# Attention rows held per group of four heads, and row maxima from 32-row products on a quarter of the array each

## The chip, the cores and the metric

The kernel runs on one core of one Trainium2 chip. Its time is the device time of one execution in microseconds. The program is one launch: eight transformer-like layers are computed one after the other on an activation of 2048 tokens by 128 channels that stays on chip.

## The reference

The input `x` is (1, 2048, 128). Each layer adds its output to `x`. Three of the layers hold the same softmax attention, and these three are what the change touches. Cut to what is computed:

```python
# layer 1, and twice more inside the two conv + mixture-of-experts layers (n_head = 16, D = 8)
qkv = h @ W                       # (T, 3*128); q and k are rotated (rope), in layer 1 also rms-normalised
scores = einsum('bqhd,bkhd->bhqk', q, k) / sqrt(D)
scores = where(causal, scores, -1e30)
p = softmax(scores, axis=-1)      # exp(s - rowmax) / sum
y = einsum('bhqk,bkhd->bqhd', p, v) @ W_out
```

The others are: a spline feed-forward layer (twice), a retention layer (`scores * decay mask`, divided by `clip(sum |scores|)`), a chunked linear attention, an RWKV recurrence, and a mixture of four experts (twice). T is 2048, there are 16 heads of 8 channels, and everything is float32 in the reference.

## The kernel before, in words

**Operands.** PE multiplies bf16 at full rate, so `qkv_stage` cuts each q and k value into three bf16 parts that add up to it (`PARTS = 3`), turns them so that channels lie on partitions, and stores them in two tensors in device memory, `q_parts` and `k_parts`, one chunk of 512 tokens at a time (line 653). A product of q and k is then all nine products of a part with a part: 9 x 8 channels = 72 rows of contraction (`KROWS`). Two more rows hold the row maximum, high and low part, against rows of -1.0 in k: the scores come out of PE with their row maximum already taken off.

**Units.** `attention_stage` (lines 726 to 1022) works in 16 units, each four heads (group g) by 512 queries (block j), in the order of the list `UNITS` at line 683. A unit has 4(j+1) steps, one for each 128 keys, so there are 160 steps. In a step PE makes the scores of 128 keys by 512 queries for the four heads (`scores`, line 905, two heads into each of two double banks), ScalarE takes the exponential (line 852, two instructions of 128x1024 a step), GpSimd zeroes what lies above the diagonal (line 828, only in the last four steps of a unit), and one step later PE multiplies by v and a column of ones (`pv`, line 918). `pv` is a float32 product and puts each head on a quarter of the array's columns (`tile_position=(0, 32 * h)`).

**Row maxima.** Ahead of its steps, a unit needs the maximum of each of its query rows: `max_unit` (PE, line 866) makes 128 queries by up to 512 keys into one of three banks (`stat`, the ring), and VectorE takes the maximum (line 965, or 962 with the mask on the diagonal block). There are 16(j+1) such maxima in a unit, 640 in all. When a unit's maxima are there, VectorE splits the result into two bf16 parts (lines 975 to 977), PE turns it (line 872, a "shift" item), VectorE copies it (line 983), and SP sends it by DMA into the two shift rows of the unit's q (line 805). PE waits for that DMA before the unit's first scores.

**The order of work.** `attention_plan` (lines 686 to 720) writes the order out by hand: each maximum, shift and output turn gets a step and a half of it, in a list `RING`. PE works a step as: scores of heads 0 and 1 of the next step, ring items of half 0, `pv` of the step before, scores of heads 2 and 3, ring items of half 1. The plan spreads the maxima evenly up to each unit's due time (three steps ahead of its first), but holds a unit's maxima back until its buffer can be loaded (`free`, line 701).

**Loads.** q and k rows lie in three buffers, one for a unit each (`unit_q`, `unit_k`, `BUFS = 3`). A unit takes 3 DMAs for k and 12 for q (each q part is repeated three times), on SP; for the first two units ScalarE's queue issues the q part. Unit u's load waits until the last scores of unit u-3 are done. SP works its list in order: load 0, the rows of -1.0, loads 1 and 2, then shift and load in turn.

**Elsewhere.** `retention_heads_stage` (from line 1400) uses `q_max` and `k_max`, 128 rows of which 72 carry the products; the others are filled once at the start (lines 134 and 142).

## Time and profile before

| | |
|---|---|
| median of 3 runs | 2924.27 us (2921.7 to 2928.33) |
| the profiled execution's own time | 2938.73 us |
| its span | 2937.0 us, mean granted clock 0.847 |
| PE busy | 2343.2 us (80%) |
| VectorE busy | 1876.7 us (64%) |
| ScalarE busy | 1434.4 us (49%) |
| GpSimd busy | 489.0 us (17%) |
| DMA queue 1 | 78.80 MB, 10.4% of 16 engines' span |

Busy is the time in which an engine had an instruction under way; a matmul counts from its start to its modelled end, so matmuls that overlap count once. The granted clock is a share of TensorE's full speed: 1.00 is 2.4 GHz and 0.50 is 1.2 GHz. Line numbers are those of the kernel's listing above. The three attention stages lie at 89 to 617, 1291 to 1826 and 2184 to 2735 us.

### The profile page before, as it was taken

How to read it: one execution, taken by the hardware profiler on the slowest of the kernel's cores; microseconds unless marked ns; L12 is line 12 of the kernel's file. 1: busy time of each engine (PE TensorE's matmuls, PEld its weight loads, DVE VectorE, ACT ScalarE, POOL GpSimd, SP SyncE). 2: the span in 40 equal slices, each digit the busy share in tenths (PEclk: the TensorE clock that was granted, in tenths of full speed). 3: DMA queues.
4: the chain of work that ended last, by engine and by line, in shares of the span. 5: the costliest groups of instructions: out<-in, count | busy, mean ns of one | idle time of the engine just before them, and what ended most of it. 6: DMA issues, size and time to landing. Idle time of an engine off the chain costs nothing. (4 is left out here: it accounts for less than half of the span.)

```text
span 2937.0 us, 41082 instructions
## 1 busy us (share of the span) xinstructions
PE 2343.2 (80%) x13556; PEld 1001.2 (34%) x13556; DVE 1876.7 (64%) x4585; ACT 1434.4 (49%) x2105; POOL 489.0 (17%) x635
## 2 busy tenths in 40 slices
PE   3499999856799439538999988996138999998898
PEld 2122232224444325422232323664122222322565
DVE  6478886655577664557888844435947888844433
ACT  4146667463699345332566655224132566654321
POOL 4100001112344325140000011000240000111100
PEclk7579999877899669766999988998565999976899
DMA  3211011101011000031110110000021211100000
GB/s 110 71 41 41 17 33 33 30 1 43 36 48 46 1 0 1 1 81 27 35 37 17 36 35 9 1 0 0 1 77 25 41 29 26 29 26 25 1 1 14
DMA packets 64351, 82.67 MB, mean 28 GB/s; under 512 B 13718, under 2 KB 49974, under 8 KB 64182
## 3 DMA queue, kind: packets, MB, share of 16 engines
q1 hardware_dynamic: 61878, 78.80, 10.4%
q10 hardware_dynamic: 2304, 1.77, 0.3%
q8 instruction: 87, 1.43, 0.2%
q14 instruction: 82, 0.67, 0.1%
HBM read 66.22 MB, written 13.63 MB: 27 GB/s over the span
## 5 line engine op out<-in xcount | busy, mean ns | idle before, releaser
L852 ACT ACTIVATE probs<-score 128x1024 f32<-128x1024 f32 x960 | 826.8, 896 | 681.4 <-PE score L905 678.1
L965 DVE TENSOR_REDUCE max_part<-stat 128x1 f32<-128x512 f32 x1152 | 723.0, 683 | 162.4 <-PE stat L866 161.0
L866 PE MATMUL stat<-unit_k,unit_q 72*128 72x512 bf16 (+3 forms) x1920 | 627.2, 392 | 158.1 <-DMA unit_q<-q_parts 110.2
L905 PE MATMUL score<-unit_q,unit_k 74*128 74x512 bf16 (+3 forms) x1920 | 554.9, 377 | 16.1 <-DMA unit_q<-row_max_turned 11.0
L918 PE MATMUL pv<-probs,v_ones 128*9 128x512 f32 (+3 forms) x3840 | 479.8, 574 | 1.4 <-ACT out_turned L843 0.5
L962 DVE CUSTOM_DVE_ANT_0 masked_scores<-stat,mask_row 128x128 f32<-128x128 f32 (+3 forms) x768 | 339.8, 486 | 192.3 <-PE stat L866 190.6
L828 POOL TENSOR_SCALAR_AFFINE_SELECT probs<-probs 128x256 f32<-128x256 f32 x384 | 155.0, 408 | 1444.5 <-ACT probs L852 1440.7
L866 PEld LDWEIGHTS stat<-unit_k,unit_q 72*128 72x128 bf16 x1920 | 196.4, 104 | 523.7 <-DVE max_part L965 186.3
L905 PEld LDWEIGHTS score<-unit_q,unit_k 74*128 74x128 bf16 x1920 | 149.3, 101 | 503.6 <-ACT probs L852 265.9
L1890 ACT ACTIVATE gate<-gate_ps 128x512 f32<-128x512 f32 x128 | 76.4, 597 | 264.2 <-PE gate_ps L1865 264.2
L1564 ACT ACTIVATE abs_act_ps<-abs_act_ps 128x1024 f32<-128x1024 f32 (+3 forms) x176 | 167.5, 952 | 27.6 <-PE abs_act_ps L1519 27.6
L1930 DVE TENSOR_TENSOR hidden<-value_ps,gate 128x512 f32<-128x512 f32 x128 | 88.5, 692 | 112.2 <-PE value_ps L1866 112.0
L1596 DVE TENSOR_REDUCE abs_part<-abs_dve_ps 128x512 f32 (+5 forms) x224 | 108.5, 514 | 45.1 <-PE abs_dve_ps L1533 43.9
L1865 PE MATMUL gate_ps<-ln_t,expert_wv 128*128 (+1 forms) x256 | 133.4, 603 | 0.0
L1866 PE MATMUL value_ps<-ln_t,expert_wv 128*128 (+1 forms) x256 | 132.4, 599 | 0.0
L1855 PEld LDWEIGHTS expert_ps<-expert_proj,hidden 128*128 128x128 f32 x1024 | 119.2, 192 | 17.7 <-issue 17.7
L1855 PE MATMUL expert_ps<-expert_proj,hidden 128*128 128x128 f32 x1024 | 119.7, 275 | 1.7 <-DVE hidden L1930 1.7
L1519 PE MATMUL abs_act_ps<-k_max,q_max 128*128 128x512 bf16 x352 | 100.6, 372 | 7.0 <-ACT abs_act_ps L1564 4.0
L918 PEld LDWEIGHTS pv<-probs,v_ones 128*9 128x9 f32 x3840 | 58.7, 89 | 130.2 <-issue 107.8
L1919 DVE SCALAR_TENSOR_TENSOR X<-expert_ps,pick,X 128x128 f32 (+1 forms) x128 | 37.5, 345 | 98.2 <-PE expert_ps L1855 98.2
L988 DVE RECIPROCAL inv_denominator<-stat 128x16 f32<-128x16 f32 x48 | 12.4, 258 | 132.2 <-PE stat L876 132.2
L1477 POOL TENSOR_SCALAR own_positive<-own_scores 128x2048 f32<-128x2048 f32 x16 | 85.7, 5359 | 0.0
(265 smaller groups left out, 2423.3 us busy)
## 6 DMA issues: line engine op xcount, KB each, us to landing
unit_k<-k_parts SPq DMA_DIRECT2D x36, 384.0 KB
unit_q<-q_parts SPq DMA_DIRECT2D x504, 24.0 KB
unit_k<-k_parts SPq DMA_DIRECT2D x36, 288.0 KB
unit_k<-k_parts SPq DMA_DIRECT2D x36, 192.0 KB
q_parts<-parts_t SPq DMA_DIRECT2D x16, 384.0 KB, 2.9
k_parts<-parts_t SPq DMA_DIRECT2D x16, 384.0 KB, 3.4
q_max<-q_parts SPq DMA_DIRECT2D x48, 96.0 KB
k_max<-k_parts SPq DMA_DIRECT2D x48, 96.0 KB
```

The costliest lines, as they stand in the source:

```text
L828: nc.gpsimd.affine_select(tile, tile, [[0, 2], [1, P]], ALU.is_ge, 0.0, base=0, channel_multiplier=-1).then_inc(cut.sem, 1)
L852: nc.scalar.activation(probs[:, n % PSLOTS, :, 0:width], sc[hp][:, :, 0:width], ACT.Exp, scale=scale).then_inc(expd.sem, 1)
L866: last = nc.tensor.matmul(out[:, 0:width], uq[0:KROWS, b, h, s * P:(s + 1) * P], uk[0:KROWS, b, h, c * BANK:c * BANK + width], start=True, ...
L905: last = nc.tensor.matmul(sc[hp][:, i, 0:BANK - f], uk[0:ROWS, b, h, kt * P:(kt + 1) * P], uq[0:ROWS, b, h, f:BANK], start=True, stop=True)
L918: last = nc.tensor.matmul(acc[32 * h:32 * h + D + 1, f:BANK], v9[:, kt, g * HG + h, :], probs[:, (2 * t + h // 2) % PSLOTS, h % 2, 0:BANK ...
L962: nc.vector.tensor_tensor_reduce(masked[:, at % 2, 0:width], ring[n % RBANKS][:, 0:width], w["mask_row"][:, BANK - width:BANK], 1.0, NEG, ...
L965: nc.vector.reduce_max(into, ring[n % RBANKS][:], AX.X).then_inc(stat_used.sem, 1)
L1564: nc.scalar.activation(ps, ps, ACT.Abs, accum_out=part[:, bass.ds(h, 1), i, 0:1]).then_inc(a_used.sem, 1)
L1596: nc.vector.tensor_reduce(part[:, bass.ds(h, 1), i, slot:slot + 1], d_ps[n % DRING][:, 0:width], AX.X, ALU.add, apply_absolute_value=True) ...
L1855: ins = nc.tensor.matmul(op[e % 2][:, s * P:(s + 1) * P], hid[:, e % 2, f, s * P:(s + 1) * P], w["expert_proj"][:, e % E, f, :], start=f = ...
L1865: nc.tensor.matmul(gp[g % 2][:], w["expert_wv"][:, e, f * P:(f + 1) * P], rhs, start=True, stop=True).then_inc(upped.sem, 1)
L1866: nc.tensor.matmul(vp[g % 2][:], w["expert_wv"][:, e, DFF + f * P:DFF + (f + 1) * P], rhs, start=True, stop=True).then_inc(upped.sem, 1)
```

## The change

`qkv_stage` stores, for the three softmax layers, two more tensors, `q_max_rows` and `k_max_rows`: for each channel the four products of two parts by two parts (`MPARTS = 2`), so four heads fill 128 rows, 32 for each head. It issues four more DMAs for each 512 tokens. The maxima are taken from these 32 rows, head h on rows 32h to 32h+31 of the array. The scores keep all nine products.

All 2048 tokens of q and of k of a group of four heads are loaded at once, into two buffers (`GBUFS = 2`), in 2 + 3 + 12 DMAs for a group; the first group is loaded in two pieces, 512 tokens first. The units run group by group, j up in even groups and down in odd ones. A group's maxima may run ahead as far as the plan puts them; only groups 2 and 3 are held back, until ten steps after the buffer's last use. The shift rows of a unit go in 4 DMAs of 8 rows instead of 2 of 16, with one semaphore for even and one for odd units. `probs` has 5 slots instead of 6, and `minus_one` borrows one of them. The retention stage has its own 72-row tensors, and the two fills at the start are gone.

```diff
+MPARTS = 2
+MROWS = MPARTS * MPARTS * 8
...
@@ qkv_stage
+    NSTORED = 16 * NQ * (2 + MPARTS * len(max_dram))
...
                     for s in range(2):
                         sp.dma_start(parts_dram[s][:, :, cols], turned_sb[:, s, :, cols]).then_inc(stored.sem, 16)
-                sp.wait_ge(stored.sem, stored.at(16 * 2 * NQ))
+                    for s, rows in enumerate(max_dram):
+                        for b in range(MPARTS):
+                            two = turned_sb[:, s, 0:MPARTS, cols] if s else bcast(turned_sb[:, s, b, cols], 1, MPARTS)
+                            sp.dma_start(rows[:, b * MPARTS:(b + 1) * MPARTS, cols], two).then_inc(stored.sem, 16)
+                sp.wait_ge(stored.sem, stored.at(NSTORED))
...
-BUFS = 3
-UNITS = [(0, 0), (0, 1), (0, 2), (0, 3), (1, 3), (2, 3), (3, 3), (1, 2), (2, 2), (3, 2), (1, 1), (1, 0), (2, 1), (2, 0), (3, 1), (3, 0)]
+GBUFS = 2
+UNITS = [(g, j if g % 2 == 0 else NQ - 1 - j) for g in range(NG) for j in range(NQ)]
+LOAD_STEPS = 10
@@ attention_plan
-    free = [min(first[u - BUFS + 1] + 3, first[u - 1] - 2) if u >= BUFS else -1 for u in range(len(UNITS))]
+    ends = [last[(g + 1) * NQ - 1] for g in range(NG)]
+    free = [ends[g - GBUFS] + LOAD_STEPS if g >= GBUFS else -1 for g, _ in UNITS]
@@ attention_stage
-    RBANKS, PSLOTS = 3, 6
+    RBANKS, PSLOTS = 3, 5
-        uq = k.sb("unit_q", [P, BUFS, HG, BANK], BF16, ctx)
-        uk = k.sb("unit_k", [P, BUFS, HG, T], BF16, ctx)
-        minus = k.sb("minus_one", [SHIFT, BANK], BF16, ctx)
+        uq = k.sb("group_q", [P, GBUFS, HG, T], BF16, ctx)
+        uk = k.sb("group_k", [P, GBUFS, HG, T], BF16, ctx)
+        mq = k.sb("max_q", [P, GBUFS, T], BF16, ctx)
+        mk = k.sb("max_k", [P, GBUFS, T], BF16, ctx)
...
+        def load_max(eng, g, cols, sig):
+            at = slice(g * HG * D, (g + 1) * HG * D)
+            for tile, rows in ((mk, max_dram[1]), (mq, max_dram[0])):
+                eng.dma_start(tile[:, g % GBUFS, cols], rows[at, :, cols].rearrange("c m t -> (c m) t")).then_inc(sig.sem, 16)
+        def load_k(eng, g, cols, sig):
             for a in range(PARTS):
                 at = slice(a * PARTS * D, (a + 1) * PARTS * D)
+                eng.dma_start(uk[at, g % GBUFS, :, cols], k_rows[g][:, :, cols]).then_inc(sig.sem, 16)
+        def load_q(eng, g, heads, cols, sig):
+            for h in heads:
+                for a in range(PARTS):
+                    at = slice(a * PARTS * D, (a + 1) * PARTS * D)
+                    eng.dma_start(uq[at, g % GBUFS, h, cols], bcast(q_rows[g * HG + h, a][:, cols], 1, PARTS)).then_inc(sig.sem, 16)
...
             def _(sp):
+                def load_group(g):
+                    if g >= GBUFS:
+                        sp.wait_ge(scored.sem, scored.at(2 * LAST[(g - GBUFS + 1) * NQ - 1] + 2))
+                    load_max(sp, g, ALL_COLS, max_loaded[g % GBUFS])
+                    load_k(sp, g, ALL_COLS, loaded[g % GBUFS])
+                    load_q(sp, g, range(HG), ALL_COLS, loaded[g % GBUFS])
...
+                load_max(sp, 0, FIRST_COLS, max_begun)
+                load_k(sp, 0, FIRST_COLS, begun)
+                load_q(sp, 0, range(HG // 2), FIRST_COLS, begun)
                 sp.wait_ge(minus_ready.sem, minus_ready.at(1))
...
+                load_max(sp, 0, OTHER_COLS, max_loaded[0])
+                load_k(sp, 0, OTHER_COLS, loaded[0])
+                load_q(sp, 0, range(HG // 2), OTHER_COLS, loaded[0])
                 load_shift(0)
+                load_group(1)
+                todo = [(item[0], 1, item[3]) for item in RING if item[2] == "shift" and item[3] > 0]
+                todo += [(LAST[(g - GBUFS + 1) * NQ - 1] + 1, 0, g) for g in range(GBUFS, NG)]
+                for _, is_shift, what in sorted(todo):
+                    if is_shift:
+                        load_shift(what)
+                    else:
+                        load_group(what)
...
             def _(act):
-                for u in range(BUFS - 1):
-                    load_q(act, u)
+                load_q(act, 0, range(HG // 2, HG), FIRST_COLS, begun)
+                load_q(act, 0, range(HG // 2, HG), OTHER_COLS, loaded[0])
...
@@ max_unit (PE)
-                    last = nc.tensor.matmul(out[:, 0:width], uq[0:KROWS, b, h, s * P:(s + 1) * P], uk[0:KROWS, b, h, c * BANK:c * BANK + width],
-                                            start=True, stop=True)
+                    rows = slice(h * MROWS, (h + 1) * MROWS)
+                    last = nc.tensor.matmul(out[:, 0:width], mq[rows, b, at:at + P], mk[rows, b, c * BANK:c * BANK + width],
+                                            start=True, stop=True, tile_position=(h * MROWS, 0))
@@ fill_ring: before a unit's first maximum
+                            if u == 0:
+                                pe.wait_ge(max_begun.sem, max_begun.at(NM))
+                            else:
+                                pe.wait_ge(max_loaded[g % GBUFS].sem, max_loaded[g % GBUFS].at(NM * (g // GBUFS + 1)))
@@ retention_heads_stage
-        qm, km = w["q_max"], w["k_max"]
+        qm, km = (k.sb(f"head_{n}", [KROWS, 2, T], BF16, ctx) for n in "qk")
```

## Rows read from the trace of the kernel before

**Rows 1.** Busy time by stretch; busy us (instructions) per engine, granted clock, DMA share, GB/s.

```profile
core 0: us, PE busy (x) PEld busy (x) DVE busy (x) ACT busy (x) POOL busy (x), PEclk, DMA share, GB/s
88.70:109.30 20.60, 0.00 (x1) 0.01 (x1) 0.97 (x2) 0.97 (x1) 2.01 (x1) 0.50 0.57 129
109.30:121.60 12.30, 7.73 (x20) 1.99 (x21) 9.25 (x39) 2.22 (x2) 0.00 (x0) 0.50 0.04 9
121.60:234.00 112.40, 103.52 (x441) 28.81 (x441) 88.46 (x220) 42.12 (x50) 9.36 (x24) 0.74 0.13 27
234.00:476.80 242.80, 236.58 (x1434) 72.82 (x1433) 200.91 (x491) 159.34 (x182) 19.54 (x49) 1.00 0.14 32
476.80:613.70 136.90, 119.61 (x733) 36.16 (x735) 68.16 (x245) 80.11 (x103) 22.41 (x57) 0.89 0.10 27
...
1681.70:1823.20 141.50, 123.35 (x733) 36.87 (x735) 68.22 (x245) 80.42 (x103) 22.41 (x57) 0.86 0.10 26
...
2572.20:2731.30 159.10, 143.52 (x733) 40.68 (x735) 68.95 (x244) 81.06 (x103) 22.45 (x56) 0.72 0.09 23
```

**Rows 2.** The same stretches of the first stage, exponentials of line 852 alone.

```profile
121.60:234.00 112.40, 40.95 (x48) 0.74 0.13 27
234.00:476.80 242.80, 157.22 (x176) 1.00 0.14 32
476.80:613.70 136.90, 77.14 (x96) 0.89 0.10 27
```

**Rows 3.** Timeline around the first stage's start; start, duration, engine, line [idle before, releaser].

```profile
84.27 0.54 SPq L653 DMA_DIRECT2D q_parts<-parts_t  x1
84.86 0.62 SPq L653 DMA_DIRECT2D k_parts<-parts_t  x1
...
88.69 19.60 ACTq L786 DMA_DIRECT2D unit_q<-q_parts  x24
...
109.30 0.50 PE L866 MATMUL stat<-unit_k,unit_q 72*128 72x128 bf16 x3 [26.59 <-DMA unit_q<-q_parts]
...
119.16 1.22 SPq L805 DMA_DIRECT2D unit_q<-row_max_turned  x2
...
121.63 1.87 PE L905 MATMUL score<-unit_q,unit_k 74*128 74x512 bf16 x4 [3.40 <-DMA unit_q<-row_max_turned]
```

**Rows 4.** Timeline of one step in the middle, clock 1.00.

```profile
402.69 0.60 PE L905 MATMUL score<-unit_q,unit_k 74*128 74x512 bf16 x2
...
403.13 0.60 PE L866 MATMUL stat<-unit_k,unit_q 72*128 72x512 bf16 x2
...
403.55 2.48 DVE L965 TENSOR_REDUCE max_part<-stat 128x1 f32<-128x512 f32 x4 [1.29 <-PE stat L866]
403.57 0.49 PE L905 MATMUL score<-unit_q,unit_k 74*128 74x384 bf16 x2
...
404.62 1.04 PE L918 MATMUL pv<-probs,v_ones 128*9 128x512 f32 x8
...
405.59 0.11 PEld L905 LDWEIGHTS score<-unit_q,unit_k 74*128 74x128 bf16 x2 [0.86 <-ACT probs L852]
```

**Rows 5.** Timeline of PE, the same pair of operations at clock 0.50.

```profile
163.26 1.90 PE L918 MATMUL pv<-probs,v_ones 128*9 128x512 f32 x8
165.09 1.03 PE L905 MATMUL score<-unit_q,unit_k 74*128 74x512 bf16 x2
```

**Rows 6.** Costliest groups of the page; busy, mean ns of one | idle before, releaser.

```profile
L918 PE MATMUL pv<-probs,v_ones 128*9 128x512 f32 (+3 forms) x3840 | 479.8, 574 | 1.4 <-ACT out_turned L843 0.5
...
L1519 PE MATMUL abs_act_ps<-k_max,q_max 128*128 128x512 bf16 x352 | 100.6, 372 | 7.0 <-ACT abs_act_ps L1564 4.0
```

**Rows 7.** Busy time by stretch, third attention stage, columns as in the first group.

```profile
2620.60:2671.80 51.20, 49.79 (x198) 14.36 (x199) 25.71 (x91) 19.11 (x25) 6.07 (x15) 0.50 0.12 30
```

**Rows 8.** Timeline of PE late in the first stage.

```profile
542.55 0.50 PE L866 MATMUL stat<-unit_k,unit_q 72*128 72x128 bf16 x3 [3.35 <-DMA unit_q<-q_parts]
```

More of the change, by code:

```diff
@@ L419, in project_stage, with qkv_stage @@
         kept.done(len(units))
-def qkv_stage(k, w, jobs, qkv, parts_dram, mode, loads=()):
+def qkv_stage(k, w, jobs, qkv, parts_dram, mode, loads=(), max_dram=()):
     nc = k.nc
@@ L667, in qkv_stage @@
             copied[a].done(NQ)
[L668 removed]
+        stored.done(NSTORED)
         step_v.done(counts[0])
@@ L750, in attention_stage @@
         acc = k.ps("pv", [P, BANK], ctx)
-        loaded = [k.counter(f"unit_loaded{b}") for b in range(BUFS)]
+        loaded, begun = [k.counter(f"group_loaded{b}") for b in range(GBUFS)], k.counter("first_block_loaded")
+        max_loaded, max_begun = [k.counter(f"max_rows_loaded{b}") for b in range(GBUFS)], k.counter("first_max_rows_loaded")
         minus_ready, minus_loaded = k.counter("minus_ready"), k.counter("minus_loaded")
-        shift_in = k.counter("shift_rows_loaded")
+        shift_in = [k.counter(f"shift_rows_loaded{n}") for n in range(2)]
         stat_full, stat_used = k.counter("stat_bank_full"), k.counter("stat_bank_used")
@@ L808, in _ @@
-                load(0)
+                    for h in range(HG):
+                        rows = uq[KROWS:ROWS, g % GBUFS, h, j * BANK:(j + 1) * BANK].rearrange("n (i q) -> n i q", q=P)
+                        sp.dma_start(rows, mxt[h * SHIFT * QC:(h + 1) * SHIFT * QC, u % 2, :]).then_inc(shift_in[u % 2].sem, 16)
+                load_max(sp, 0, FIRST_COLS, max_begun)
+                load_k(sp, 0, FIRST_COLS, begun)
+                load_q(sp, 0, range(HG // 2), FIRST_COLS, begun)
                 sp.wait_ge(minus_ready.sem, minus_ready.at(1))
@@ L814, in _ @@
                 load_shift(0)
-                for u in range(NU):
-                    if u + 1 < NU:
-                        load_shift(u + 1)
-                    if u + BUFS < NU:
-                        load(u + BUFS)
+                load_group(1)
[6 more added lines that the diff above has]
+                        load_group(what)
@@ L899, in scores @@
                     u, kt = STEPS[t]
-                    b, f = u % BUFS, first_col(t)
+                    g, j = UNITS[u]
+                    b, f = g % GBUFS, first_col(t)
                     if hp == 0 and t == FIRST[u]:
-                        pe.wait_ge(shift_in.sem, shift_in.at(SHIFT * 16 * (u + 1)))
+                        if u == 0:
+                            pe.wait_ge(begun.sem, begun.at(NL))
+                        else:
+                            pe.wait_ge(loaded[g % GBUFS].sem, loaded[g % GBUFS].at(loads_of(g)))
+                        pe.wait_ge(shift_in[u % 2].sem, shift_in[u % 2].at(HG * 16 * (u // 2 + 1)))
                     for i in range(2):
                         h = 2 * hp + i
-                        last = nc.tensor.matmul(sc[hp][:, i, 0:BANK - f], uk[0:ROWS, b, h, kt * P:(kt + 1) * P], uq[0:ROWS, b, h, f:BANK],
+                        last = nc.tensor.matmul(sc[hp][:, i, 0:BANK - f], uk[0:ROWS, b, h, kt * P:(kt + 1) * P], uq[0:ROWS, b, h, j * BANK + f:(j + 1) * BANK],
                                                 start=True, stop=True)
@@ L972, in row_max @@
                     j = UNITS[u][1]
-                    nt = HG * QC
-                    high, low = mxb[:, u % 2, 0:nt], mxb[:, u % 2, nt:2 * nt]
+                    high, low = (mxb[:, u % 2, :].rearrange("p (h n i) -> p n h i", n=SHIFT, i=QC)[:, n] for n in range(SHIFT))
+                    top = mx[:].rearrange("p (h i) -> p h i", i=QC)
                     step(nc.vector.tensor_reduce(mx[:], mpart[:, u % 2, :, 0:j + 1], AX.X, ALU.max))
-                    step(nc.vector.tensor_copy(high, mx[:]))
-                    nc.vector.tensor_tensor(low, mx[:], high, ALU.subtract).then_inc(max_ready.sem, 1)
+                    step(nc.vector.tensor_copy(high, top))
+                    nc.vector.tensor_tensor(low, top, high, ALU.subtract).then_inc(max_ready.sem, 1)
                 def shift_unit(n, u):
                     if u >= 2:
-                        dve.wait_ge(shift_in.sem, shift_in.at(SHIFT * 16 * (u - 1)))
+                        dve.wait_ge(shift_in[u % 2].sem, shift_in[u % 2].at(HG * 16 * (u // 2)))
                     rows = mxt.shape[0]
@@ L1000, in _ @@
                 counts.append(chain.n)
-        for b in range(BUFS):
-            loaded[b].done(NL * len([u for u in range(NU) if u % BUFS == b]))
+        begun.done(NL)
+        max_begun.done(NM)
+        for b in range(GBUFS):
+            loaded[b].done(NL * NG // GBUFS)
+            max_loaded[b].done(NM * NG // GBUFS)
         minus_ready.done(1)
         minus_loaded.done(16)
-        shift_in.done(SHIFT * 16 * NU)
+        for sig in shift_in:
+            sig.done(HG * 16 * NU // 2)
         stat_full.done(len(RING))
```

72 lines of the change are left out of this document (22 added, 50 removed).

## The prediction

> **What bounds the kernel now.** The change touches three stages, so I read each one alone. The table of busy time by stretch comes first [rows 1]: cut one attention stage at its first maximum, its first score, step 24, step 112 and its last exponential. The exponentials counted in each stretch fix the steps (two a step): 48, 176 and 96, so 24, 88 and 48 steps [rows 2]. One stage is 20.6 + 12.3 + 112.4 + 242.8 + 136.9 = 525.0 us. The reader is to see four regimes.
> - *Start* (20.6 us): no engine works. The timeline says why: ScalarE's queue issues 24 DMAs in 19.60 us, 0.82 us each, and PE's first maximum waits for the last of them [rows 3]. 12.3 us later come the first scores, behind maxima, row maximum and the shift DMA.
> - *Ramp* (24 steps, 4.68 us each): clock 0.74, VectorE 88.5 of 112.4 us. It is fed six maxima a step at 0.62 us, and PE at half clock is nearly as slow.
> - *Middle* (88 steps, 2.76 us each): clock 1.00, PE busy 236.6 of 242.8 us, VectorE 200.9. PE is the bound. The timeline of one step [rows 4] gives its terms: two products of 512 columns take 0.44 us from start to start (402.69 to 403.13), so 0.22 each; from `pv` to the weights of the next score it is 0.97 us (404.62 to 405.59). At half clock the same stretch is 1.83 us [rows 5]. What streams doubles and what is fixed does not: 2 x 0.97 - 1.83 = 0.11 us is fixed, the step from quarter-column products back to whole-array ones. So `pv` streams 0.86 us, and a change of tiling costs some 0.1 us. A full step is 8 x 0.22 + 0.86 + 2 x 0.1 = 2.82 us; 2.76 with the shorter diagonal steps.
> - *Tail* (48 steps, 2.85 us each though mostly short): PE waits up to 3.35 us for q rows [rows 8], since a unit's buffer is freed late; the clock falls to 0.50 after such waits, and the mean is 0.89, 0.86 and 0.72 in the three stages, which take 136.9, 141.5 and 159.1 us [rows 1].
>
> **Sum, against the profiled execution** (2938.73 us, span 2937.0; 14.5 above the median 2924.27, most of it, I think, the third tail's clock, which gives 159.1 us where the others take 139 [rows 1]).
>
> *Storing the extra rows.* After the last 512 tokens of each softmax `qkv_stage` four more DMAs follow the two there. These take 0.54 and 0.62 us to issue [rows 3], so four are 2.3 us; their 1 MB more lands meanwhile or just after. I take +3 us a stage (bounds +2.3 and +5), fully exposed: attention starts when the stores have landed.
>
> *Start.* The first maximum waits for two DMAs only, so it can start about 2 us after the stage does, not 20.6. But the first scores then wait for something else: before the first shift SP issues 10 DMAs of max and k rows, 12 of q, and the rows of -1.0. At 0.59 us (the stores' mean and more) the 23 take 13.6 us, against 12 DMAs, 9.8 us, on ScalarE's queue. Four shift DMAs (0.6 each) and 1.3 us to land (119.16 + 1.22 to 121.63 [rows 3]) make 17.3, with a microsecond for the queue's backlog 18.3 us, where it was 32.9. Gain 14.6 us a stage (bounds 8, if the shift rows land behind 3 MB of others, and 18). Group 1's 17 DMAs follow, 10 us of issue, while VectorE works through unit 1's 32 maxima (20 us), so unit 1's shift finds SP free.
>
> *Ramp.* Working the plan through, steps 12 to 23 hold 67 maxima instead of 61, 6 x 0.62 = 3.7 us more for VectorE, taken off later stretches. At half clock PE's step gets lighter where maxima overlap, and its changes of tiling make it less dense. I take +4 us (bounds -10 and +20).
>
> *Middle.* Heads follow each other in the plan, so two maxima of a half step lie on different row quarters and in different banks. Do such tiles run at the same time? The nearest row is `pv`: 3840 instructions of 574 ns are 2204 us of matmul in 479.8 us busy [rows 6], 4.6 at once, on column quarters. I take it that row quarters do the same: a pair costs one product, 0.22, if both banks are free. Against this stands the order of work: score, maxima, `pv`, score, maxima, score is now three tilings, so five changes a step where there were two. A full step: 0.88 + 0.86 + 2 x 0.22 + 5 x 0.1 = 2.68 us. VectorE's four maxima take 2.48 us [rows 4], and with three banks the second of a pair will often wait for it and not overlap; I take back 0.11 us of the 0.14. Middle: -3 us a stage. Bounds: 2.55 a step (VectorE's floor with no loss), -19 us; 0.88 + 0.86 + 0.88 + 0.5 = 3.12 with no overlap at all, +26 us.
>
> The Trainium skill speaks against this edit on one page, TensorEngine Tiling (Array Packing), section Key Properties: changing the tiling mode drains TensorE. The trace agrees, with 0.11 us fixed beside `pv` [rows 5]; by that rule alone the edit loses 3 x 0.1 us a step. The page TensorE: Matmul & The Clock Gate, Part 3, gives a measured 3.07 times for four row tiles, by which the pairs would win it back; no row of this case has row tiles.
>
> *Tail.* With all of a group's rows on chip no maximum waits for a buffer. The plan by hand puts four maxima in each step to 128, then two. Steps 112 to 119: 8 x 2.7 = 21.6 us. Of 120 to 159, 24 are full: one maximum in each half, so 0.88 + 0.86 + 0.44 + 0.5 = 2.68 us, 64.3 us. 16 are diagonal, with 5/8 of the columns (0.55 + 0.54 us): with maxima and changes of tiling 2.0 us, and without maxima ScalarE holds them, at up to 2 x 0.89 us (157.22 by 176 [rows 2]); I take 1.9 in the mean, 30.4 us. Sum 116.3 us, if the clock holds, as it does in the middle. Before: 136.9, 141.5, 159.1. Gain 20.6 + 25.2 + 42.8 = 88.6 us (bounds: 105 us a tail, 122; 140 a tail, 18).
>
> *At nothing.* The group loads move 17 DMAs to steps 40 and 80, 20 steps before their rows are read; shift 10, planned for step 84 and needed at 92 (21 us), stands behind 10 us of issue, and if cover fails costs a few us once a stage. Five slots of `probs`: the exponential of heads 2 and 3 needs `pv` of two steps back, which stands ahead of its scores on PE anyway. Retention's 72 rows: 512 columns cost PE 372 ns on 128 rows [rows 6], and 0.22 from start to start on 74 and 72 [rows 4]; columns set it. The two fills lay beside the first loads.
>
> Per stage: 3 - 14.6 + 4 - 3 = -10.6; three times, -31.8; with the tails -88.6: -120.4. 2938.7 - 120.4 = 2818.3 us. Against the median, whose third tail is likely shorter, the gain is some 15 us less but starts 14.5 lower: about the same. I say 2820.
>
> **Rivals.**
> - *A, the changes of tiling eat the change.* Row quarters don't overlap, or the pairs never find two free banks: 3.12 us in full steps of the middle. +26 instead of -3, so 29 x 3 = 87 us back: 2907 us. For it: VectorE's 2.48 of 2.82 us leaves little room in three banks. Against: `pv`'s overlap.
> - *B, slower: the clock stays at half.* Drains and overlapped products leave PE less dense. At clock 0.50 a full step with pairs is 1.76 + 1.72 + 0.88 + 0.5 = 4.86 us instead of 2.68, so 2.2 us each. The gain of 120 us is gone when 55 of the 480 steps more than before run so; at 80 steps more the time is 2820 + 176 = 2996 us, which I take. For it: in the third stage the clock stayed at 0.50 for 51.2 us with PE busy 49.8 [rows 7], and the ramp stays at 0.50 for long; at half clock PE's streaming share of a full step falls from 5.24 of 5.44 us, 96%, to 4.36 of 4.86, 90%, and it was such dense work that ran before the clock rose. Against: in the first stage's middle it held at 1.00 for 243 us [rows 1], and the waits of several us, after which it fell [rows 8], are gone.
> - *C, better.* Pairs overlap fully and the clock rises sooner: middle -19, ramp -8, tail 108 (-28 more than 116.3, over three -25), start as above: 3 x (3 - 14.6 - 8 - 19) - 113.5 = -229: 2709 us; halfway there 2765.
>
> **How the numbers follow.** Forecast 0.60 (its own range 2775 to 2865), A 0.13, B 0.14, C 0.13. Range 2745 to 2925: it takes in A and half of C, and leaves B and C's end out, some 0.2. Faster by over 0.2% (about 6 us, what a measurement of this kernel can tell): forecast, C and most of A, 0.83; same: 0.03; slower: B, 0.14.
>
> **What would show it.** In the profile after: first maximum about 2 us and first score 18 us behind the stage's start; no `stat <- DMA` wait longer than a microsecond after it; maxima of one half step starting some ns apart (overlap) or 0.22 us apart (rival A), with 0.1 us before and behind them; 2.7 to 2.75 us a step in steps 24 to 111; a tail near 117 us in all three stages at a clock near 1.00. It is wrong if a stage's middle shows a clock under 1.00 (B), or if VectorE, not PE, ends most waits of the middle at under 2.6 us a step (C).

## The result

The changed kernel takes 3246.8 us (median of 4 runs, 3181.4 to 3414.9), the kernel before 2925.1 us (4 runs, 2921.7 to 2928.3): a ratio of 1.093, 95% interval [1.084, 1.102]. Some runs of one kernel are slower at a lower clock, and every ratio here is taken from the faster ones (of the changed kernel, 3181.4 and 3210.9 us), while medians are of all runs. The prediction was 2820 us, and its range ended at 2925. The outcome is rival B, which had a chance of 0.14.

The changed kernel's own runs spread by 7%, and the mean clock spreads with them: 0.748 in the run of 3181 us, 0.680 in that of 3415. The profiled one (span 3280.9 us, clock 0.715; before 2937.0, 0.847) lies between.

The table of busy time by stretch, cut as in [rows 1]: stage start, first maximum, first score, step 24, step 112, last exponential; then the tails of the second and third stage, and the retention stage. Columns as there.

```profile
93.17:97.26 4.09, 0.00 (x0) 0.00 (x1) 0.97 (x2) 0.00 (x0) 2.02 (x1) 0.50 0.55 148
97.26:122.58 25.32, 6.39 (x21) 1.62 (x21) 9.34 (x39) 3.18 (x2) 0.00 (x0) 0.50 0.67 159
122.58:259.60 137.02, 131.62 (x448) 22.80 (x448) 91.85 (x229) 42.49 (x50) 9.71 (x24) 0.50 0.08 17
259.60:593.10 333.50, 330.06 (x1446) 60.71 (x1445) 202.05 (x526) 161.47 (x185) 25.89 (x64) 0.65 0.08 21
593.10:720.80 127.70, 125.29 (x714) 28.56 (x717) 70.24 (x196) 83.30 (x101) 15.62 (x39) 0.92 0.01 1
...
1909.10:2027.60 118.50, 116.34 (x714) 27.84 (x718) 70.20 (x197) 82.98 (x101) 15.61 (x39) 1.00 0.00 1
...
2883.50:3075.60 192.10, 191.44 (x715) 30.34 (x718) 71.95 (x195) 86.96 (x100) 15.76 (x39) 0.52 0.00 1
...
863.80:1098.10 234.30, 216.58 (x1920) 106.32 (x1920) 153.94 (x321) 184.41 (x369) 93.54 (x38) 0.84 0.11 41
```

Against [rows 1] the reader is to see one column, the clock. The ramp has 0.50 where it had 0.74 and takes 137.0 us for 112.4. The middle has 0.65 where it had 1.00, and takes 333.5 for 242.8. PE is busy 330 of 333.5 us, so no new wait costs this; VectorE's busy time is 202 us where it was 201. The middles of the second and third stage took 317.8 us at 0.69 and 323.9 at 0.68. The tail is the cleanest case. The same 48 steps, with the same instructions, take 118.5 us at clock 1.00 and 192.1 at 0.52. Over the three attention stages the sum is 1917.5 us for 1614.4, +303. The retention stage takes 234.3 us for 211.9, +22, and the stages that compute q, k and v +17. These three make 342 of the 344 us between the two spans.

The page's line of the clock in 40 slices, and the groups that answer to [rows 6]: busy time, mean ns of one, idle time before and its releaser.

```profile
PEclk7555568986679769755576799996655867555699
...
L928 PE MATMUL score<-group_q,group_k 74*128 74x512 bf16 (+3 forms) x1920 | 710.6, 465 | 25.9 <-DMA group_q<-row_max_turned 23.4
L880 PE MATMUL stat<-max_k,max_q 32*128 32x512 bf16 (+3 forms) x1920 | 586.3, 469 | 100.1 <-DMA max_q<-q_max_rows 74.9
L941 PE MATMUL pv<-probs,v_ones 128*9 128x512 f32 (+3 forms) x3840 | 628.1, 737 | 0.7 <-ACT out_turned L856 0.5
...
L1546 PE MATMUL abs_act_ps<-head_k,head_q 72*128 72x512 bf16 x352 | 115.7, 420 | 4.6 <-ACT abs_act_ps L1591 2.7
```

`pv`, which the change doesn't touch, went from 574 to 737 ns an instruction: the same instructions at a lower clock. Retention's product went from 372 to 420 ns when it lost 56 rows of zeros.

The start of the first stage, PE and then SP's queue, as [rows 3] of before.

```profile
97.26 0.29 PE L880 MATMUL stat<-max_k,max_q 32*128 32x128 bf16 x3 [15.83 <-DMA max_q<-q_max_rows]
...
111.77 0.61 PE L880 MATMUL stat<-max_k,max_q 32*128 32x512 bf16 x3 [8.55 <-DMA max_q<-q_max_rows]
113.24 0.27 PE L886 MATMUL stat<-ident,row_max_parts 128*32 128x128 bf16 x1 [0.87 <-DVE max_part L988]
122.58 1.86 PE L928 MATMUL score<-group_q,group_k 74*128 74x512 bf16 x4 [9.07 <-DMA group_q<-row_max_turned]
```

```profile
86.47 2.25 SPq L652 DMA_DIRECT2D q_max_rows<-parts_t  x2
88.76 1.49 SPq L652 DMA_DIRECT2D k_max_rows<-parts_t  x2
...
101.44 2.03 SPq L782 DMA_DIRECT2D max_q<-q_max_rows  x1
...
114.44 2.72 SPq L813 DMA_DIRECT2D group_q<-row_max_turned  x4
```

The stage starts at 93.17 us and the first score comes 29.4 us later, not 18.3. In PE's list three maxima of unit 1 stand ahead of the transpose (L886) that turns unit 0's row maxima. VectorE had these ready at 105.2 us, but the three maxima waited 8.55 us for rows whose load was issued only at 101.44, and the transpose ran at 113.24. Then the shift rows landed 5.4 us after their last issue (114.44 + 2.72 to 122.58), where the prediction took 1.3 us.

Now single steps. At clock 1.00 the small costs of the sum were there. This is PE's timeline late in the first stage's middle, as [rows 4].

```profile
584.61 1.04 PE L941 MATMUL pv<-probs,v_ones 128*9 128x512 f32 x8
585.59 0.61 PE L928 MATMUL score<-group_q,group_k 74*128 74x512 bf16 x2
586.13 0.39 PE L880 MATMUL stat<-max_k,max_q 32*128 32x512 bf16 x2
586.45 0.60 PE L928 MATMUL score<-group_q,group_k 74*128 74x512 bf16 x2
586.99 0.69 PE L880 MATMUL stat<-max_k,max_q 32*128 32x512 bf16 x2
587.61 1.05 PE L941 MATMUL pv<-probs,v_ones 128*9 128x512 f32 x8
588.59 0.61 PE L928 MATMUL score<-group_q,group_k 74*128 74x512 bf16 x2
```

At 586.13 two maxima take 0.32 us together until the next score (0.22 and one change of tiling), so row quarters do run at once; at 586.99 the second waits for its bank and the pair takes 0.62. Scores to maxima is 0.54, two products and 0.1. `pv` to score is 0.98, as before. This step takes 3.00 us from `pv` to `pv`, the one before it 2.63 and the one after it 3.01. And the same at half clock, where most of the ramp and middle ran:

```profile
287.32 1.90 PE L941 MATMUL pv<-probs,v_ones 128*9 128x512 f32 x8
289.15 1.03 PE L928 MATMUL score<-group_q,group_k 74*128 74x512 bf16 x2
290.12 0.50 PE L880 MATMUL stat<-max_k,max_q 32*128 32x384 bf16 x2
290.55 1.03 PE L928 MATMUL score<-group_q,group_k 74*128 74x512 bf16 x2
291.52 0.61 PE L880 MATMUL stat<-max_k,max_q 32*128 32x512 bf16 x2
292.06 1.90 PE L941 MATMUL pv<-probs,v_ones 128*9 128x512 f32 x8
```

One step takes 4.74 us from `pv` to `pv`, with no gap. Rival B's price was 4.86.

### The profile page after: what moved, and what is told of

Same layout as the page of the kernel before. It is cut to its first block and busy times, and to the rows that moved or that the text cites. A ratio compares the mean times of both kernels' runs of the same rounds, so it can differ in the third digit from the quotient of the medians.

```text
span 3280.9 us, 40762 instructions
## 1 busy us (share of the span) xinstructions
PE 2744.1 (84%) x13556; PEld 932.6 (28%) x13556; DVE 1897.5 (58%) x4584; ACT 1454.9 (44%) x2105; POOL 483.4 (15%) x634
## 5 line engine op out<-in xcount | busy, mean ns | idle before, releaser
L865 ACT ACTIVATE probs<-score 128x1024 f32<-128x1024 f32 x960 | 841.1, 896 | 997.7 <-PE score L928 996.3
L988 DVE TENSOR_REDUCE max_part<-stat 128x1 f32<-128x512 f32 x1152 | 733.0, 685 | 382.1 <-PE stat L880 380.9
L928 PE MATMUL score<-group_q,group_k 74*128 74x512 bf16 (+3 forms) x1920 | 710.6, 465 | 25.9 <-DMA group_q<-row_max_turned 23.4
L880 PE MATMUL stat<-max_k,max_q 32*128 32x512 bf16 (+3 forms) x1920 | 586.3, 469 | 100.1 <-DMA max_q<-q_max_rows 74.9
L941 PE MATMUL pv<-probs,v_ones 128*9 128x512 f32 (+3 forms) x3840 | 628.1, 737 | 0.7 <-ACT out_turned L856 0.5
L985 DVE CUSTOM_DVE_ANT_0 masked_scores<-stat,mask_row 128x128 f32<-128x128 f32 (+3 forms) x768 | 347.3, 488 | 253.2 <-PE stat L880 250.9
L880 PEld LDWEIGHTS stat<-max_k,max_q 32*128 32x128 bf16 x1920 | 128.3, 96 | 712.8 <-DVE max_part L988 256.1
L928 PEld LDWEIGHTS score<-group_q,group_k 74*128 74x128 bf16 x1920 | 118.7, 104 | 701.3 <-issue 504.9
L1546 PE MATMUL abs_act_ps<-head_k,head_q 72*128 72x512 bf16 x352 | 115.7, 420 | 4.6 <-ACT abs_act_ps L1591 2.7
```

The lines of the kernel that those rows point to most:

```text
L865: nc.scalar.activation(probs[:, n % PSLOTS, :, 0:width], sc[hp][:, :, 0:width], ACT.Exp, scale=scale).then_inc(expd.sem, 1)
L880: last = nc.tensor.matmul(out[:, 0:width], mq[rows, b, at:at + P], mk[rows, b, c * BANK:c * BANK + width], start=True, stop=True, tile_pos ...
L928: last = nc.tensor.matmul(sc[hp][:, i, 0:BANK - f], uk[0:ROWS, b, h, kt * P:(kt + 1) * P], uq[0:ROWS, b, h, j * BANK + f:(j + 1) * BANK], ...
L941: last = nc.tensor.matmul(acc[32 * h:32 * h + D + 1, f:BANK], v9[:, kt, g * HG + h, :], probs[:, (2 * t + h // 2) % PSLOTS, h % 2, 0:BANK ...
L985: nc.vector.tensor_tensor_reduce(masked[:, at % 2, 0:width], ring[n % RBANKS][:, 0:width], w["mask_row"][:, BANK - width:BANK], 1.0, NEG, ...
L988: nc.vector.reduce_max(into, ring[n % RBANKS][:], AX.X).then_inc(stat_used.sem, 1)
```

## The experiments

**The two halves of the change, apart.** First, rows kept per group, maxima as before on 72 rows of the whole array.

```
-rows = slice(h * MROWS, (h + 1) * MROWS)
-matmul(out[:, 0:width], mq[rows, b, at:at + P], mk[rows, b, c * BANK:...], tile_position=(h * MROWS, 0))
+matmul(out[:, 0:width], uq[0:KROWS, b, h, at:at + P], uk[0:KROWS, b, h, c * BANK:...])
```

> The changed kernel with one part undone: groups of four heads stay on chip, with the new order of units, but the maxima come from the nine products on 72 rows of the whole array, as before, and no extra rows are stored. Theory (the 32-row maxima keep TensorE's clock down): granted clock 1.00 through the middle of all three stages, 2.78 us a step there, a tail near 117 us in each stage, and a total of 2800 to 2880 us, faster than the kernel before. Rival (the group order or the group loads, a long ramp for example, keep the clock down): clock near 0.72 over the span and over 3100 us, as the changed kernel.

Measured: 2859.7 us (2844.6 to 2901.7), before 2925.0; ratio 0.978 [0.971, 0.986]. The form of the maxima, with the extra rows that it needs, turns a gain of 65 us into a loss of 320. Its first stage, ramp, middle and tail (here and below a stretch can start with the first exponential, about 1 us behind the first score):

```profile
119.80:233.60 113.80, 104.36 (x445) 28.92 (x443) 91.11 (x229) 42.24 (x50) 9.68 (x24) 0.75 0.08 20
233.60:473.30 239.70, 230.89 (x1445) 73.30 (x1444) 198.55 (x528) 156.00 (x185) 25.65 (x65) 1.00 0.08 21
473.30:590.20 116.90, 113.33 (x714) 32.97 (x717) 69.52 (x196) 83.28 (x101) 15.60 (x39) 0.96 0.01 1
```

Then the other half: maxima in row quarters, in the order, buffers and loads of before.

```
+mq = k.sb("max_q", [P, BUFS, BANK], BF16, ctx)
+mk = k.sb("max_k", [P, BUFS, T], BF16, ctx)
-matmul(out[:, 0:width], uq[0:KROWS, b, h, s * P:(s + 1) * P], uk[0:KROWS, b, h, ...])
+matmul(out[:, 0:width], mq[rows, b, s * P:(s + 1) * P], mk[rows, b, ...], tile_position=(h * MROWS, 0))
```

> The other part alone: the loads, buffers and order of units of the kernel before, but the maxima from the stored 32-row products on a row quarter each (two more DMAs a unit, four more stores for each 512 tokens). Theory (32-row maxima keep the clock down): clock near 0.70 over the span, over 3150 us. Rival (it takes the new order of units too): clock as before, and 2920 to 2980 us.

Measured: median 3207.9 us (3141.2 to 3310.0), before 2925.0. The runs spread by 5%, and the lowest is still 200 us above any of before. Ramp and middle of its first stage:

```profile
133.40:266.70 133.30, 127.90 (x441) 22.09 (x438) 89.17 (x221) 42.50 (x50) 9.75 (x24) 0.51 0.16 33
266.70:521.70 255.00, 250.24 (x1433) 57.26 (x1433) 201.19 (x487) 160.04 (x182) 19.16 (x48) 0.97 0.18 43
```

With the old order of units, too, the row quarters lower the clock, but not everywhere. Ramps ran at 0.51, 0.58 and 0.50 and tails at 0.70, 0.65 and 0.66, while the middles of the three stages ran at 0.97, 1.00 and 0.97 and took 249 to 255 us. So the long half clock in the changed kernel's middle needs the quarters together with the rest of the change (order of units, buffers and loads). What in that rest does it, no run here separates.

**Is it density, or the rows in use?** Rival B was argued with drains and gaps. Here all maxima of one head follow each other, so neighbours share a quarter. They then run one after the other, and PE has fewer gaps.

```
-maxima = [("max", u, (h, s, c)) for s in range(QC) for c in range(j + 1) for h in range(HG)]
+maxima = [("max", u, (h, s, c)) for h in range(HG) for s in range(QC) for c in range(j + 1)]
```

> The changed kernel with the maxima in another order: all of a head's maxima follow each other (head, row tile, key block), so that two in a half step lie on the same quarter of PE's rows and run one after the other, 0.22 us each at full clock and 0.43 at half. Nothing else differs. Theory 1 (overlap leaves PE less dense, and density is what raises the clock): the streaming share of a full step at half clock goes from 88 to 91%, the clock rises in the ramp as before the change, and the total falls under 3050 us in spite of 0.4 us more a step. Theory 2 (products on 32 rows count for little, however dense): the clock stays at 0.50 at least as long, a step at half clock takes 5.4 us instead of 4.5, and the total is over 3300 us.

Measured: median 3604.0 us (3534.0 to 3631.5), clock 0.653. In its first stage's middle PE was busy 372.0 of 373.5 us at a clock of 0.62. In the second stage the middle took 435.6 us with PE busy throughout, all of it at 0.50; that is 4.95 us a step, not 5.4. So "less dense" is refuted: work without a gap and with fewer rows in use at once has a lower clock.

**The clock by itself.** A program with nothing but PE's products: stretches of one pattern after rests of some 10 us. It leaves out the layers. It ran once, so the first six patterns were each measured once.

```
whole(rows):    matmul(bank[:, 0:512], B[0:rows, 0:128], B[0:rows, 512:1024])
row_tile(q):    the same on rows 32q to 32q+31, tile_position=(32 * q, 0)
step(maxima):   2 x whole(74); maxima(); pv(); 2 x whole(74); maxima()
```

> Not the reference's computation: the input is copied to the output, and beside that PE runs 18 stretches of 25 to 65 us, each after some 10 us of rest, of products of random bf16 or float32 data that nobody reads. Stretches in order: 120 products of 512 columns on 72 rows of the whole array; 120 on 128 rows; 120 on one quarter of 32 rows; 120 rounds of four quarters; 30 pv (float32, four column quarters); 36 rounds of two whole-array products and two on one row quarter; then three times a row of four: 12 steps as before (2 scores, 2 maxima of 72 rows, pv, 2 scores, 2 maxima), 14 steps as after the change (pairs of maxima on two row quarters), 12 steps with both maxima of a pair on one quarter, 12 steps with 72-row maxima cut in two column halves that run together (as many changes of tiling as after the change). Theory 1 (density): the clock rises in all dense stretches, 32 rows too, and stays at 0.50 or rises late only in the steps as after. Theory 2 (rows count): it stays at 0.50 in the stretches of 32-row products alone, rises in the column halves, and not in steps with 32-row maxima. Rival 3 (changes of tiling hold it down): steps as before rise, all three other kinds of step do not, and the two-and-two round does not.

Rows of the table by stretch, PE first, the clock third from the right. In this order: 120 products of 72 rows; 120 of 128 rows; 120 on one quarter of 32 rows; 4 x 120 on four quarters in turn; `pv` alone; 2 of 74 rows and 2 on one quarter, in turn; twelve steps as before; fourteen as in the change; twelve with both maxima of a pair on one quarter; twelve with 72-row maxima in column halves.

```profile
17.70:68.40 50.70, 50.68 (x119) 18.07 (x120) 0.00 (x0) 0.00 (x0) 0.00 (x0) 1.00 0.00 0
78.80:106.70 27.90, 27.89 (x119) 12.19 (x120) 0.00 (x0) 0.00 (x0) 0.00 (x0) 1.00 0.00 1
116.80:167.50 50.70, 50.65 (x119) 17.35 (x120) 0.00 (x0) 0.00 (x0) 0.00 (x0) 0.50 0.00 0
177.90:205.80 27.90, 27.87 (x476) 12.23 (x480) 0.00 (x0) 0.00 (x0) 0.00 (x0) 0.92 0.01 2
215.90:243.20 27.30, 27.29 (x236) 6.28 (x240) 0.00 (x0) 0.00 (x0) 0.00 (x0) 0.93 0.00 1
253.60:322.40 68.80, 68.80 (x144) 9.08 (x144) 0.00 (x0) 0.00 (x0) 0.00 (x0) 0.50 0.00 0
332.70:371.00 38.30, 38.29 (x191) 10.32 (x192) 0.00 (x0) 0.00 (x0) 0.00 (x0) 0.87 0.00 1
381.10:448.30 67.20, 67.17 (x222) 8.21 (x222) 0.00 (x0) 0.00 (x0) 0.00 (x0) 0.50 0.00 0
458.70:526.30 67.60, 67.60 (x192) 7.58 (x192) 0.00 (x0) 0.00 (x0) 0.00 (x0) 0.50 0.00 0
536.60:602.20 65.60, 65.59 (x238) 8.86 (x240) 0.00 (x0) 0.00 (x0) 0.00 (x0) 0.53 0.00 0
```

In the first stretch the clock column can't be right: 120 products in 50.7 us are 0.42 each, as in the third at 0.50, where the full level gives 0.21. I go by the durations there, and so at the beginning of the second, where 11 products took 4.6 us. Every stretch kept PE busy without a gap. 72 rows alone stay at half clock (1.2 GHz), 128 rows leave it (27.9 us for as many); one quarter alone stays, four at once leave it. Steps as before reach 0.87 and in two repetitions 0.95; steps as in the change stay at 0.50 in all three. So dense work isn't enough: the stretches in which all 128 rows multiply left the half clock, and those of 72 and of 32 rows alone did not. The steps as before have 72- and 74-row products and still rose, but they also have `pv`, which works on 128 rows and rose when alone.

Theory 1 is refuted. Theory 2 missed one point: it had the column halves rise, and they rose only after 62 of 65.6 us. Changes of tiling aren't needed to hold the clock down, since the first stretch has none. But what rival 3 said of the kinds of step is what came: those as before rose, the other three and the round of two and two didn't. These stretches don't tell whether changes of tiling help to hold the clock down beside the rows; the next run does for the kernel.

The Trainium skill says otherwise on its page TensorE: Matmul & The Clock Gate, Part 1: there the clock follows how busy TensorE has been, and sustained work raises it. The first and third stretch here, with PE busy 50.7 of 50.7 us and no rise, don't agree.

**Does it carry back into the kernel?** The change complete, but the scores contract over 128 rows (those above 74 filled with zeros).

```
+nc.vector.memset(uq[64:P, b].bitcast(F32), 0.0)      # and group_k, on gpsimd
-matmul(sc[hp][:, i, 0:BANK - f], uk[0:ROWS, b, h, ...], uq[0:ROWS, b, h, ...])
+matmul(sc[hp][:, i, 0:BANK - f], uk[0:P, b, h, ...], uq[0:P, b, h, ...])
```

> The changed kernel, its maxima on row quarters and its pairs as they are, but the scores' contraction goes over 128 rows of the array instead of 74: rows 74 to 127 of q and k hold zeros, filled by VectorE and GpSimd beside the first loads of a stage. Theory (the clock follows how many rows products use): the steps as after the change stayed at 0.50 for 67 us in the stretches measured alone, where steps with more rows in use rose; with full-height scores the clock rises in the ramp of all three stages as in the kernel before, each attention stage falls from 605 to 682 us to 490 to 530 us, and the total to 2860 to 2960 us. Rival (the changes of tiling or the overlap, not rows, hold it down): clock and time as the changed kernel, over 3150 us.

Measured: 2902.6 us (10 runs, 2878.9 to 2939.3), before 2919.3; ratio 0.994 [0.990, 0.997]. The middle of its first stage:

```profile
234.80:480.00 245.20, 238.04 (x1445) 58.61 (x1445) 199.02 (x527) 156.17 (x186) 25.72 (x65) 1.00 0.11 29
```

Multiplying zeros takes back 340 of the changed kernel's 3247 us, and this middle takes 245.2 us for 333.5. This is the decisive run: the changes of tiling, the pairs and PE's order of work are the changed kernel's (only the first loads of a stage are ordered anew around the fills), and more rows multiply. All three middles and tails ran at 1.00; the ramps at 0.73 to 0.79, where the kernel before had 0.72 to 0.74.

**Retention's rows.** Rows kept alone as above, with retention's products back on 128 rows.

```
-qm, km = (k.sb(f"head_{n}", [KROWS, 2, T], BF16, ctx) for n in "qk")
+qm, km = w["q_max"], w["k_max"]      # 128 rows, filled once
```

> The rows kept on chip alone (maxima on 72 rows of the whole array), and the retention stage's products on 128 rows again, zeros and -1.0 below the 72, as in the kernel before. Theory (rows): the retention stage takes 212 us again instead of 230, as its clock is back at 1.00, and the total is 2830 to 2850 us. Rival (the retention stage's 18 to 22 us come from something else, its tensors' place for one): total 2850 to 2870, retention at 230.

Measured: 2821.8 us (2813.1 to 2832.8), ratio 0.967 [0.961, 0.973]. Two retention stages, with 72 rows (rows kept alone) and with 128:

```profile
733.60:963.60 230.00, 212.17 (x1920) 103.82 (x1920) 153.43 (x320) 183.94 (x368) 93.51 (x37) 0.87 0.11 41
```

```profile
734.90:946.80 211.90, 191.93 (x1920) 93.70 (x1920) 151.71 (x320) 181.79 (x368) 93.52 (x37) 0.98 0.12 45
```

18 us for 56 rows that add nothing to the result, at a clock of 0.98 for 0.87. The total is 8 us under the theory's range; the stage is as forecast. Of all the kernels here, the six with this stage on 128 rows took 212 us for it. The six with the same code on 72 rows took 230, 234, 238, 256, 257 and 271 us, at clocks of 0.87 down to 0.69. The 230 above is the best of them, and why they differ so much isn't settled.

**Both on 128 rows,** maxima still on 72 of the whole array.

> As rows_kept_retention_128, and the scores on 128 rows too, with zeros. Theory (rows): the clock rises within some 20 us of a stage's first scores instead of 40 and more, and stays up in the tail; each attention stage 475 to 495 us instead of 495 to 504; total 2770 to 2820 us, faster than both kernels. Rival (VectorE bounds the ramp anyway, so the clock is worth nothing there): total as rows_kept_retention_128 within 10 us.

Measured: 2786.7 us (2781.7 to 2792.4), ratio 0.956 [0.951, 0.961]; again beside other runs, 2786.5 (2785.2 to 2788.9). That is 35 us under the run before, so the rival is refuted. In the profiled executions the three attention stages fell by 47 us: 30 in the ramps, whose clock was 0.85 to 0.88 instead of 0.73 to 0.76, 6 in the tails, and 11 at the start, before the first scores. The last isn't the clock: the first loads of a stage are ordered anew around the fills.

> The same kernel as rows_kept_128_rows, on the same chip as first_turn_first and beside the same runs of the kernel before, so that the two can be compared: 2782 to 2792 us.

**What are the quarters worth when the clock is up?** The whole change, with scores and retention on 128 rows.

> The whole change with every other product put on 128 rows: maxima stay on one 32-row quarter a head, as in the change, scores and retention run on 128 rows (rows above filled with zeros; retention fills them once at its start). Beside rows_kept_128_rows, which differs in the form of the maxima, this prices the form at the clock it then gets. Theory (the clock is held by the products on 128 rows, and at full clock the pairs of quarters give no gain): attention 505 to 515 a stage as in scores_on_128_rows (its middle took 245.2 us at clock 1.00, 2.79 a step, against 239.8 with maxima on 72 rows of the whole array), retention 212 to 215 instead of 257, so about 2902 - 42 = 2860 us. Rival (row quarters keep the clock down in the rest of the kernel too): retention stays at 230 to 257, 2880 to 2905 us.

Measured: 2881.6 us (2878.4 to 2888.9), ratio 0.987 [0.984, 0.989]; retention 212.3 us. Ramp and middle of the first stage, quarters first and then whole-array maxima (the repetition):

```profile
126.20:238.70 112.50, 97.66 (x440) 21.26 (x444) 90.91 (x229) 41.66 (x50) 9.75 (x24) 0.77 0.08 18
238.70:485.00 246.30, 235.66 (x1423) 58.50 (x1445) 198.83 (x527) 156.28 (x186) 25.74 (x64) 0.99 0.10 29
```

```profile
115.70:221.20 105.50, 93.62 (x438) 26.94 (x443) 90.46 (x228) 41.96 (x50) 9.68 (x24) 0.85 0.11 22
221.20:461.00 239.80, 228.37 (x1424) 73.30 (x1444) 198.38 (x528) 156.00 (x185) 25.82 (x65) 1.00 0.08 21
```

With every other product on 128 rows, quarters cost 95 us: 24 us an attention stage and 6 to 8 us in each stage that stores the extra rows. In the first stage the middle takes 6.5 us more (2.80 us a step for 2.73), the ramp 7, the tail 6 and the start 2. The middles and tails compare at one clock (0.99 to 1.00). The ramps don't: theirs was 0.77, 0.68 and 0.83, for 0.84, 0.88 and 0.88. On VectorE nothing changed, and PE is busy 7 us longer in the middle: the pairs overlap, but not often enough to pay for three more changes of tiling. The theory's 2860 us was missed by 22, and the total lies in the rival's range, but the rival's cause is refuted by retention's 212.3.

**Column halves** instead of row quarters: 72 rows stay in use, and changes of tiling are as many as in the change.

```
+for x in range(0, P, 64):
+    matmul(out[x:x + 64, 0:width], uq[0:KROWS, b, h, at + x:at + x + 64], uk[0:KROWS, ...], tile_position=(0, x))
```

> The rows kept on chip alone, with each maximum's product cut in two halves of the array's columns that run together, 72 rows each: as many changes of tiling a step as in the changed kernel, no row tiles. Theory (rows): steps of this kind stayed at 0.50 for 62 us of 66 when measured alone and then rose, so the clock rises late in each stage but rises, at steps 20 to 30, and once up holds; at full clock a step is 3 x 0.1 us longer than the 2.76 before, 3.05 in the middle; total 2940 to 3040 us. Rival (changes of tiling alone explain the changed kernel): over 3150 us with the clock at 0.50 for hundreds of us in a stage.

Measured: median 3002.5 us (2967.2 to 3019.9), before 2919.3. The middle of its first stage ran at clock 0.97 and took 261.5 us. The other two middles ran at 1.00 and took 255.0. So with as many changes of tiling the kernel kept its clock in the middle, and the changes alone don't explain the change's loss. This is the weakest of the clock's results, though: in the clock program twelve steps of this pattern stayed at a mean of 0.53 for 65.6 to 66.2 us, in all three repetitions, so how far 72 rows in halves hold the clock depends on something these runs don't separate. Its retention stage, on 72 rows, took 271.4 us, the longest of the six named above, and accounts for 41 us of the total over rows kept alone.

**The start.** In the kernel with rows kept and 128 rows throughout, unit 0's transpose goes ahead of unit 1's maxima.

```
-stream += maxima[:LATE] if u else maxima
+late = LATE if u > 1 else 0
+stream += maxima[:late] if u else maxima
```

> Everything as in rows_kept_128_rows (rows kept per group, all products of scores, maxima and retention on 128 rows); only the order on PE at a stage's start changes: the transpose that turns unit 0's row maxima now stands ahead of unit 1's first three maxima, not behind them. In rows_kept_128_rows the row maxima were ready at 104.5 us, but the transpose ran at 108.84, behind maxima that waited until 107.36 for unit 1's q rows. Theory (the missing part of the start is this place in PE's queue): the transpose at 104.6, the shift's DMAs at 105.8 to 108.5, the first score 4.2 us earlier, at 109.7; three stages, 12 to 13 us: 2774 us. Rival (SP's queue or the landing of 3 MB of rows sets it): the shift rows land behind the others, the first score moves by under 1 us and the time stays at 2786. What could take some back: unit 1's first maxima move behind the first scores, so its row maximum is later by some us.

Measured: 2786.2 us (2780.5 to 2789.9) beside 2786.5. Rows of PE's timeline:

```profile
104.53 0.29 PE L897 MATMUL stat<-ident,row_max_parts 128*32 128x128 bf16 x1 [2.00 <-DVE row_max_parts L1013]
110.92 1.49 PE L939 MATMUL score<-group_q,group_k 128*128 128x512 bf16 x3 [6.10 <-DMA group_q<-row_max_turned]
```

The transpose ran 5.1 us sooner than in the repetition (109.62) and the first score 4.1 us (115.03), so the place in PE's queue was real. The median didn't follow. Neither theory's number came out: the score moved, and of the 12 us nothing is left in the medians. The shift rows took 3.2 us to land after their last issue, where they took 1.6. In the profiled executions the first scores came 4.2, 3.5 and 4.7 us sooner after the first maximum in the three stages, but the second stage's ramp took 109.4 us at clock 0.84 instead of 104.5 at 0.88 and gave its share back. Whether that is the rule isn't shown.

## Why the prediction was wrong

The step that failed is the middle's "-3 us a stage", and with it every term that stood on the clock: the tails' "if the clock holds, as it does in the middle", and the ramp's +4. Rival B named the outcome and priced a step well (4.86 us; 4.74 in the timeline above, 4.80 in the clock program's fourteen in 67.2 us). Its time of 2996 us was 250 too low all the same, by the count of steps and not by their price: it took 80 steps more at half clock. By the granted clock the three attention stages spent some 1320 us at the half level, where it was some 380 before (first maximum to last exponential; clocks 0.66, 0.70 and 0.60, for 0.90, 0.89 and 0.85). As a rough estimate, the 940 us more are 196 steps of 4.8 us, and 2820 + 196 x 2.2 = 3251 us. And B got its chance of 0.14 from the wrong cause: I argued it with the share of the time in which PE streams, 96% to 90%. The runs show that the share doesn't decide: at 99.6% busy on single quarters the clock was lower still, and scores on 128 rows, 54 of them zeros, raised it again with the changes of tiling in place. The change took the maxima from 72 rows to 32, and pairs to 64 at best. What stays open is how rows, order of work and changes of tiling together set the time at which the clock rises: quarters in the old order of units left the middle at 0.97 to 1.00.

Point by point:
- *Storing, +3 us a stage.* +4.3, +6.4 and +6.5. The two stores of `q_max_rows` took 2.25 us to issue together, 1.1 each, where I took 0.6; the two of `k_max_rows`, without a broadcast, took 0.75 each.
- *Start, -14.6.* -3.5 us to the first score (29.4 for 32.9), then -5.7 and -6.1 in the other stages. The working had the shift behind SP's queue only; its transpose stood behind unit 1's maxima on PE, which waited for late rows, and its rows landed 4 us later than taken. Making the start 4 us shorter brought no time in the one kernel where it was tried, so this term was worth less than its size as well.
- *Ramp, +4.* +24.6, +23.1 and +22.8, at clocks of 0.50, 0.50 and 0.53. With rows kept alone 114.9 us for 112.4 in the first stage; VectorE's extra maxima were as worked out (91.9 us for 88.5, where I had 3.7 more).
- *Middle, -3.* +90.7, +75.0 and +81.1 us, the largest part of the loss. Overlapping pairs and 0.1 us a change were right; the step worked out for the quarters, 2.73 us (2.76 less the 0.03 left of the gain), was not reached even at full clock: 2.80 with quarters, and 2.73 without them. The second of a pair waited for a bank oftener than I took back. That part is rival A in small: 246.3 us for 242.8, where whole-array maxima in the new order took 239.8.
- *Tails, 116.3 us each.* 118.5 us at clock 1.00, 127.7 at 0.92, 192.1 at 0.52. The sum was right at full clock, but its condition, "if the clock holds", failed in two stages of three. With rows kept alone 116.9, 112.4 and 112.2, with no wait for q rows as in [rows 8]: 96 of the 113 us that its attention stages gained, the rest being start and middle.
- *Retention's 72 rows at nothing.* +22.4 us. "Columns set it" is true of one product at one clock; with 72 rows instead of 128 the stage ran at 0.84 instead of 0.98.

The evidence lay in the profile: in [rows 7] the clock stayed at 0.50 while PE was busy 49.8 of 51.2 us on 72- and 74-row products, and the retention stage of before, on 128 rows, ran at 0.98. I put the first down to density, as a sign for rival B, and didn't look at the second. Alone they prove nothing: the middles of before ran 72- and 74-row products at 1.00.

## What to carry to other kernels

Where PE is the bound, ask of a new form of product not only how many columns it streams but how many of PE's rows multiply while it does: work that is busy without a gap can still sit at 1.2 GHz (here for 435.6 us). Filling the contraction up to 128 rows with zeros cost nothing per product here (two scores take 0.54 us with the change of tiling behind them on 74 rows and on 128, and the middle 239.7 and 239.8 us) and was worth more than the rows saved; here retention's zeros took the ratio to before from 0.978 to 0.967, and the scores' to 0.956. Test the two halves of a change apart: the rows kept on chip were a good change (0.978, and 0.956 with 128 rows), hidden by a bad one.

## What the runs showed of the hardware

- 120 products of 512 columns took 50.7 us on 72 rows and 27.9 on 128 rows, each with PE busy throughout; on one quarter of 32 rows 50.7, and 480 on four quarters 27.9 (each measured once).
- Steps of PE with 74-row scores, `pv` and 72-row maxima ran at a mean clock of 0.87 to 0.95; with 32-row maxima they stayed at 0.50 for the whole 67.2 us, three times out of three.
- The same stage of retention took 212 us in six kernels with its products on 128 rows, and 230 to 271 us in six with 72.
- Products on different row quarters run at once: a pair took 0.32 us with its change of tiling, where one product of 512 columns streams 0.22.
- A change of tiling is about 0.1 us of PE whichever way it goes (score to maxima 0.54 for two products of 0.22, `pv` to score 0.98).
- A DMA that doubles rows on the way took 1.1 us of SP's time to issue, plain ones of the same stage 0.67 to 0.77. Plain ones elsewhere took from 0.34 to 2.03 us, so the form isn't all of it.
